# Cross-attention and FFN kernel: dequantisation started at the context maxima over two pairs of PSUM banks

## What is computed

```
q = layernorm(x); k = v = ctx
proj(a, W, b) = a @ W.T + b          -> 16 heads x 8 x 4 ("sup"), for Wq, Wk, Wv (512 x 512)
interfere(a)  = a + 0.1*amp*einsum(a, interference[h])      on the last axis (4)
weights = softmax(q.k / sqrt(8)) per head and sup; out = (weights @ v) @ Wo.T + bo
x = x + out
w_gu = sc[g]*(wq - (zq[g]+1))        4-bit, 512 x 2752, 4 groups
w_d  = the same, 1376 x 512, 10 groups
x = x + (silu(gate)*up) @ w_d        gate, up = layernorm(x) @ w_gu
```

## Time and profile before

| | us |
|---|---|
| median of 3 runs | 906.57 (904.34 to 906.67) |
| the profiled execution | 906.32 |
| its span, first to last instruction | 904.6 |
| mean granted TensorE clock | 0.902 of 2.4 GHz |

### The profile page before, as it was taken

The page is one execution under the profiler, slowest core; times in us unless marked ns, Lnnn a source line. Parts: engine busy times, 40 slices in busy tenths (PEclk is TensorE's granted clock), DMA queues, the critical chain, the costliest instruction groups (busy, mean ns, idle before and its releaser), DMA issues.

```text
span 904.6 us, 23874 instructions
## 1 busy us (share of the span) xinstructions
PE 772.6 (85%) x9953; PEld 562.3 (62%) x9953; DVE 510.2 (56%) x1013; ACT 438.3 (48%) x806; POOL 326.8 (36%) x290
## 2 busy tenths in 40 slices
PE   5306457766799999999999999999999999999898
PEld 5303323322278857876787778677857885787484
DVE  6987745554465646655574556456645663644421
ACT  1426355676365526662555455454635462655120
POOL 6732324555314530543064114412431352144220
PEclk9758655565599999999999999999999999999999
DMA  8900113222101011002100110011001100010000
GB/s 248 292 23 1 50 32 89 69 56 63 32 25 28 3 49 50 3 3 71 28 2 14 60 28 3 13 60 28 2 21 52 28 2 25 3 27 3 24 1 23
DMA packets 20702, 36.98 MB, mean 41 GB/s; under 512 B 3374, under 2 KB 7602, under 8 KB 20592
## 3 DMA queue, kind: packets, MB, share of 16 engines
q1 hardware_dynamic: 20604, 35.48, 13.5%
HBM read 26.56 MB, written 4.19 MB: 34 GB/s over the span
## 4 chain that ended last, share of the span: by engine, by line
PE 67%; DVE 15%; ACT 8%; issue 6%; DMA 2%; SPq 1%; DVEq 0%; ACTq 0%; POOL 0%
PE bank L511 16%; PE bank L526 13%; PE bank L482 9%; PE bank L492 9%; PE bank L644 4%; DVE nmf L1166 4%; PE bank L638 3%; PE bank L661 3%; ACT arena L849 3%; PE bank L619 2%; PE bank L459 2%; DVE arena L1094 2%; DMA arena<-in_L_xattn_Wo 2%; DVE arena L985 2%; PE bank L443 2%
## 5 line engine op out<-in xcount | busy, mean ns | idle before, releaser
L511 PE MATMUL bank<-arena,WGU 128*128 128x256 f16 (+1 forms) x2112 | 247.0, 274 | 1.4 <-DVE arena L709 1.4
L511 PEld LDWEIGHTS bank<-arena,WGU 128*128 128x128 f16 (+1 forms) x2112 | 206.2, 100 | 27.5 <-DVE arena L709 1.6
L1368 POOL TENSOR_TENSOR arena<-arena 128x512 f16<-128x512 f32 x128 | 147.0, 1173 | 190.5 <-ACT arena L856 190.5
L482 PE MATMUL bank<-arena,WT 128*128 128x256 f16 x768 | 91.3, 281 | 40.4 <-DVE arena L709 39.1
L526 PE MATMUL bank<-WD,arena 128*128 128x512 f16 (+1 forms) x528 | 121.1, 379 | 0.0
L849 ACT ACTIVATE arena<-bank,small 128x512 f32<-128x512 f32 x128 | 89.1, 776 | 58.3 <-PE bank L644 58.3
L1355 POOL TENSOR_TENSOR arena<-arena 128x512 f16<-128x512 f32 (+1 forms) x48 | 51.7, 1077 | 172.2 <-ACT arena L829 172.2
L482 PEld LDWEIGHTS bank<-arena,WT 128*128 128x128 f16 x768 | 76.9, 101 | 54.6 <-issue 43.1
L492 PE MATMUL bank<-WT,arena 128*128 128x512 f16 x384 | 88.0, 387 | 1.8 <-DVE arena L707 1.8
L526 PEld LDWEIGHTS bank<-WD,arena 128*128 128x128 f16 (+1 forms) x528 | 49.4, 98 | 53.2
L1166 DVE TENSOR_REDUCE nmf<-bank 128x8 f32<-128x512 f32 x128 | 79.4, 682 | 4.4 <-PE bank L619 4.2
(11 more groups left out here) (157 smaller groups left out, 1068.8 us busy)
## 6 DMA issues: line engine op xcount, KB each, us to landing
arena<-in_L_ffn_qweight_gu SPq DMA_DIRECT2D x8, 688.0 KB, 5.4
arena<-arena SPq DMA_DIRECT2D x32, 144.0 KB, 3.0
WT<-in_ctx SPq DMA_DIRECT2D x8, 512.0 KB, 15.1
arena<-in_ctx SPq DMA_DIRECT2D x8, 512.0 KB, 3.7
arena<-in_x SPq DMA_DIRECT2D x8, 512.0 KB, 3.6
out_y<-arena SPq DMA_DIRECT2D x16, 256.0 KB, 2.1
arena<-in_L_ffn_qweight_down SPq DMA_DIRECT2D x10, 256.0 KB, 3.4
arena<-in_L_xattn_Wk SPq DMA_DIRECT2D x1, 1024.0 KB, 6.6
```

The costliest lines, as they stand in the source:

```text
L482: mm = e.matmul(jb[:, g2 * TOK:(g2 + 1) * TOK], WT[:, w, sp, kb, g * P:(g + 1) * P], src[:, mp, kb, :], start=(n == 0), stop=(n == 11))
L511: mm = e.matmul(pb[0:m, i * TOK:(i + 1) * TOK], WGU[:, sp, kb, half * INTER + fb * P:half * INTER + fb * P + m], x2T[:, mp, kb, :], start= ...
L1368: e.tensor_tensor(phl[:, a, 1, :], pring[:, a, :], phl[:, a, 0, :], ALU.subtract).then_inc(S["p_lo"], 1)
```

## The change

What each part does:

1. **Where the units run.** ND + 5 = 40 ticks. Twenty come early, at new places: one each after the fourth, sixth and eighth context maximum (ctx4, ctx6, ctx8), three at `scales`, two each at `w0` and `w1`, five each at `keys` (after the K projection) and `values` (after the V rows). The other twenty stay in slots: one in each of slots 0 and 1, four in each batch (slot positions 0, 2, 3, 3), two at the end.
2. **Lags.** VectorE does int(n) and w(n - 3), TensorE unit n - 2, ScalarE scaled(n - 2) and hi(n - 4), GpSimd conv(n) and lo(n - 5).
3. **Banks.** The first TWO_PAIRS = 17 units alternate between GB/UB and the JB pair, and wait for `d_w` one unit less. The folds then use only the four AB banks, one after the other.
4. **Conversion** of the integers to bf16 moves from ScalarE to GpSimd (`pool_dequant_conv`).
5. **Wide tables.** The gate/up scales and zero points are loaded over 128 and 32 partitions, split there by VectorE, and written to their table rows by 12 + 4 DMAs from SBUF to SBUF. `dve_zeros` and the gate/up parts of `act_scale_part` are gone.
6. **Own scales for dequantisation.** The maxima of the two scale inputs are reduced by a PARTITION_ALL_REDUCE of their own, early (`MXQ`, `MRQ`); the large one remains.
7. **Reordering of Wo** moves from VectorE to ScalarE. The gate/up one-hot moves from GpSimd to VectorE; the down one-hot stays on GpSimd, in four parts around a subtraction.
8. The order of the loads on SyncE changes.

```diff
-TICKS = ND + 3
-FIRST_SLOT = 2
-TICK_ENDS = [0] * FIRST_SLOT + [TICKS * (k + 1) // (SLICES - FIRST_SLOT) for k in range(SLICES - FIRST_SLOT)]
+TICKS = ND + 5
+TICKS_AT = {"ctx4": 1, "ctx6": 1, "ctx8": 1, "scales": 3, "w0": 2, "w1": 2, "keys": 5, "values": 5}
+BATCH_TICKS = [0, 1] + [slot[j] for slot in IN_BATCH for j in (0, 2, 3, 3)] + AT_TAIL[:2]
+TWO_PAIRS = sum(TICKS_AT[p] for p in PLACES[:PLACES.index("values") + 1]) - 3
...
+            e.wait_ge(S["sc_zeroed"], 2)
+            e.wait_ge(S["wide_ready"], 1)
+            for i in range(PARTS):
+                for g in range(GROUPS_GU):
+                    e.dma_start(sc3_gu[32 * i + g:32 * i + g + 1, :], sc3w[32 * g:32 * g + 32, i, :]).then_inc(S["sc_table"], 16)
+            e.wait_ge(S["zwide_ready"], 1)
+            for g in range(GROUPS_GU):
+                e.dma_start(z_gu[g:g + 1, :], zw[8 * g:8 * g + 8, :]).then_inc(S["z_table"], 16)
+            for c in range(4, NCHUNK):
+                load_ctx_max(e, c)
...
+            for place in ("ctx4", "ctx6", "ctx8", "scales"):
+                pe_ticks(e, place)
+            e.wait_ge(S["fold_evicted"], 4)
+            for t in range(TILES):
+                pe_transpose_tile(e, -1, f"cT{t}", cin, S["ctx_loaded"], 16)
+            pe_ticks(e, "w0")
+            pe_ticks(e, "w1")
...
+            return (JB[0], JB[1]) if n < TWO_PAIRS and n % 2 == 0 else (GB, UB)
...
-            reached(e, S["d_w"], n)
+            reached(e, S["d_w"], n - 1 if n < TWO_PAIRS else n)
...
                 pe_project(e, 1, 1, AB[1], cxT)
             if first:
+                pe_ticks(e, "keys")
                 e.wait_ge(S["wlo_done"], 2)
                 for t in range(TILES):
                     pe_rows(e, 2, t, AB[2 + t], cxT, S["proj_done"])
+                pe_ticks(e, "values")
...
+            for place in ("ctx4", "ctx6", "ctx8", "scales"):
+                act_ticks(e, place)
             e.wait_ge(S["scale_ready"], 1)
             act_whi(e, 0)
             act_hi(e, -1, "cT0"), act_hi(e, -1, "cT1")
+            act_ticks(e, "w0")
             act_whi(e, 1)
+            act_ticks(e, "w1")
...
             for c in range(NCHUNK):
                 e.wait_ge(S[f"ctxm_loaded{c}"], 16)
                 ins = e.tensor_reduce(MXC[:, c:c + 1], cmax_st[:, c], AX_X, ALU.max, apply_absolute_value=True)
+                if c in (3, 5):
+                    dve_ticks(e, f"ctx{c + 1}")
...
+            for n in ticks(place):
+                dve_dequant_int(e, n)
+                dve_dequant_w(e, n - 3)
...
+            e.wait_ge(S["maxq_ready"], 1)
+            e.partition_all_reduce(MRQ, MXQ, P, ABSMAX).then_inc(S["maxq_all"], 1)
+            e.wait_ge(S["sc_high"], 1)
+            e.tensor_tensor(rest_d[0:96, :], scd[0:96, :], sc3_d[0:96, :], ALU.subtract).then_inc(S["sc_rest"], 1)
+            e.wait_ge(S["sc_high"], 2)
+            for i in range(4):
+                pool_hot_d(e, i)
+                if i == 1:
+                    e.tensor_tensor(rest_d[0:64, :], rest_d[0:64, :], sc3_d[0:64, :], ALU.subtract).then_inc(S["sc_rest"], 1)
+            for place in ("ctx4", "ctx6"):
+                pool_ticks(e, place)
             e.wait_ge(S["max_ready"], 1)
             e.partition_all_reduce(MR, MX, P, ABSMAX).then_inc(S["max_all"], 1)
+            pool_ticks(e, "ctx8")
             pool_ln(e, "x", 0)
...
+            for n in ticks(place):
+                pool_dequant_conv(e, n)
+                pool_dequant_lo(e, n - 5)
```

More of the change, by code:

```diff
@@ L83, with ticks @@
 PARTS = 3
-TICKS = ND + 3
-FIRST_SLOT = 2
-TICK_ENDS = [0] * FIRST_SLOT + [TICKS * (k + 1) // (SLICES - FIRST_SLOT) for k in range(SLICES - FIRST_SLOT)]
-def ticks(slot):
-    return range(TICK_ENDS[slot - 1] if slot else 0, TICK_ENDS[slot])
+TICKS = ND + 5
+PLACES = ["ctx4", "ctx6", "ctx8", "scales", "w0", "w1", "keys", "values"] + list(range(SLICES))
+TICKS_AT = {"ctx4": 1, "ctx6": 1, "ctx8": 1, "scales": 3, "w0": 2, "w1": 2, "keys": 5, "values": 5}
+BATCH_TICKS = [0, 1] + [slot[j] for slot in IN_BATCH for j in (0, 2, 3, 3)] + AT_TAIL[:2]
+assert sum(TICKS_AT.values()) + len(BATCH_TICKS) == TICKS
+TICKS_AT.update((k, BATCH_TICKS.count(k)) for k in BATCH_TICKS)
+TWO_PAIRS = sum(TICKS_AT[p] for p in PLACES[:PLACES.index("values") + 1]) - 3
+def ticks(place):
+    before = sum(TICKS_AT.get(p, 0) for p in PLACES[:PLACES.index(place)])
+    return range(before, before + TICKS_AT.get(place, 0))
 def width(block):
@@ L189, in build @@
         eye4 = take(16, F32)
+        early = [take(2048, F32) for _ in range(KB)]
+        bvx = take(2048, F32)
+        inter_all, inter_own, own = early[0][:, 0:HEADS * SUP * SUP], early[0][:, 256:512], early[1][:, 0:4 * SUP]
+        zraw_d = early[1][:, 4 * SUP:4 * SUP + DM // 8].bitcast(U32)
+        zint_d, scd = early[2].bitcast(U32), early[3]
+        rest_d = take(2048, F32)
         wop = [take(2048, F32) for _ in range(KB)]
-        bvx = take(2048, F32)
-        inter_all, inter_own, own = wop[0][:, 0:HEADS * SUP * SUP], wop[1][:, 0:HEADS * SUP * SUP], wop[2][:, 0:4 * SUP]
         take, pos = carver(max(pos[0], body0_end))
@@ L247, in build @@
         BMASK = small[:, 108:124].rearrange("p (w v k) -> p w v k", w=2, v=2)
+        MXQ, MRQ, BDQ, SCQ = (small[:, 124 + 2 * i:126 + 2 * i] for i in range(4))
         GM = small[:, 100:101]
@@ L539, in ffn_slice @@
                 if first:
-                    for n in ticks(k):
-                        pe_dequant(e, n - 1)
+                    pe_ticks(e, k)
                     return
@@ L833, in act_slot @@
             if first:
-                for n in ticks(k):
-                    act_dequant(e, n)
+                act_ticks(e, k)
             else:
@@ L869, in act_chunk @@
                 act_whi(e, 2)
+                act_ticks(e, "keys")
             else:
@@ new lines, in dve_ticks, with dve_zeros_d @@
+        def dve_ticks(e, place):
+            for n in ticks(place):
+                dve_dequant_int(e, n)
+                dve_dequant_w(e, n - 3)
+        def dve_zeros_d(e):
+            e.wait_ge(S["z_loaded"], 16)
+            for k in range(8):
+                ins = e.tensor_scalar(ap(zint_d, 0, GROUPS_D, k, [(8, DM // 8)]), zraw_d[0:GROUPS_D, :], 4 * k, 15,
+                                      ALU.logical_shift_right, ALU.bitwise_and)
+            link(e, ins)
+            e.tensor_scalar(z_d[0:GROUPS_D, 0:DM], zint_d[0:GROUPS_D, 0:DM], -1.0, -1.0, ALU.mult, ALU.add).then_inc(S["zd_ready"], 1)
@@ L1155, in dve_slot @@
             if first:
-                for n in ticks(k):
-                    dve_dequant_int(e, n)
-                    dve_dequant_w(e, n - 1)
+                dve_ticks(e, k)
             else:
@@ L1358, in pool_slot @@
             if first:
-                for n in ticks(k):
-                    pool_dequant_lo(e, n - 3)
+                pool_ticks(e, k)
             else:
@@ L1370, in pool_chunk @@
         def pool_chunk(e, c, first=False, last=False):
+            if first:
+                pool_ticks(e, "keys")
+                e.wait_ge(S["bo_loaded"], 16)
+                e.wait_ge(S["wlo_done"], 3)
+                pool_xres(e, 0)
+                pool_ticks(e, "values")
             pool_slot(e, c, 0, first)
```

277 lines of the change are left out of this document (161 added, 116 removed).

## The result

The changed kernel takes 915.39 us against 905.84 us for the kernel before in the same series. That is the median of four executions, 914.57, 915.12, 915.67 and a slow one of 1954 us, which the ratio leaves out. The ratio is 1.0104, with a 95% interval of 1.0084 to 1.0125: a small difference, but clear of noise. The profiled execution took 914.57 us, 8.25 us more than that of before, and its span is 912.8 us.

The account below looks back on a forecast made before the run. TensorE bounds the kernel from the first Wo; before it, waits between engines decide. Setup -2.9, to K +11.8, to Q +19.0, to scores +5.6, batches -26.4: +7.1 on 906.32 gives 913.4 us; range 895 to 926, the forecast's own 909 to 918.

Parts of the forecast that it names:

- K to Q: From K to Q projection: 45.2 us for 26.2, with ten units added and 0.4 us a unit for port locks.
- The later stretch and the frame: From the first Wo on, TensorE is nearly full and untouched: 664.3 us kept; everything to win or lose lies before.
- The reordering on ScalarE: Setup: the 32 Wo copies cost ScalarE 0.2 us each, 6.4 us, and take 14.4 us off VectorE.
- The chain of GpSimd: Setup: configuration changes around all-reduces cost 7.1 us each, three on the path; second all-reduce at 51.2, scale_ready at 57.0.
- rival 1: GpSimd before the second all-reduce: configuration changes cost nothing, scale_ready at 46.4, total 902.7 us; chance 17%.
- The last fold is out at about 44, at most 52: Setup: with ScalarE's Wo copies after the third fold's copies, the last fold leaves at about 44 us, at most 52.
- Two pairs of banks don't help here: scale_ready to K (22.0 us for 10.1): no help, since engines run in order and w comes a tick late.
- Q to scores and the batches: Q to first scores 18.1 us for 12.5, with two units between; the four batches 105.1 us for 131.5.
- the one unit of slot 0 waits for a w behind the maxima: Start of each batch: from maxima to the unit's turn 5.7 us against 6.2 before, so no gain.
- ring of 3.2 us for units 17 to 34: Sign: units 17 to 34 still take the 3.2 us round of TensorE, ScalarE and VectorE; under 2.3 us in keys.
- Rival 2: Batches and after Q: units cost their busiest engine's 1.8 us, not 3.2; up to 20 us saved, 896 us; chance 13%.
- rival 4: GpSimd's conversions and low parts lock VectorE's ports, 1 us a unit more over ten; reload up to 12 us; 925 us; 14%.

Follow-up runs that it names:

- x6: The kernel before with only the 32 copies that reorder Wo moved to ScalarE: 893.10 us, ratio 0.9862.
- x2: The changed kernel with the early all-reduce of the scale inputs' maxima replaced by a memset constant: 918.54 us, ratio 1.0143 to the kernel before.
- x10: x1 with the scale inputs' maxima in the large all-reduce, and gate/up one-hot, scales and conversions 0 and 1 behind it: 920.38 us, ratio 1.0159 to before.
- x1: The changed kernel with ScalarE's second down-scale part after the first fold's copies, not before the bias copies: 911.41 us, ratio 1.0062 to the kernel before.
- x4: The changed kernel with all units on one pair of banks (TWO_PAIRS = 0): 936.32 us, ratio 1.0333 to the kernel before.
- x14: The changed kernel with VectorE doing w(n - 2) instead of w(n - 3) in the slots: 887.85 us, ratio 0.9800 to the kernel before.
- x5: The changed kernel with the conversion of the integers on ScalarE instead of GpSimd: 923.24 us, ratio 1.0191 to the kernel before.
- x7: The changed kernel with the ten ticks of keys and values, and their piece loads, back in the slots: 928.25 us, ratio 1.0254 to the kernel before.
- x13: x7 with w(n - 2) instead of w(n - 3) in the slots: 893.00 us, ratio 0.9854 to the kernel before.
- x11: x10 with eight small zero-point shifts moved behind the context maxima and rstd ahead of the scales ticks: 911.76 us, ratio 1.0052 to the kernel before.
- x12: x11 with w(n - 2) instead of w(n - 3) in the slots: 884.10 us, ratio 0.9754 to the kernel before.

## Why the prediction was right, and where its working was not

The forecast of 913.4 us, slower, held (915.39; the profiled execution 914.57), and the mechanism that it names, early units that cost more ahead of Q than they save in the batches, is what the stretches show. That it came within 2 us is in part luck: K came 4.6 us later than forecast and the stretch from K to Q was 3.6 us shorter, and two of its signs, the first high part at 62 to 64 and K at 77 to 81, failed (67.75 and 83.57). Step by step:

- **The later stretch and the frame.** 663.2 us against 664.3. Right.
- **The reordering on ScalarE.** 0.2 us a copy; it took 6.51 us for 32. Right. x6 prices the part at 12.6 us.
- **The chain of GpSimd.** Three stalls ahead of the second all-reduce, predicted at 50.8 to 51.2, came at 51.89, and `scale_ready` at 58.41 for 57.0. Right, and rival 1 with its price of nothing per stall fell. But that such a stall is pure loss, as its sum has it, fell too, in x2 and x10.
- **"The last fold is out at about 44, at most 52".** Wrong, 57.9. The step "they start after the third fold's copies" took the folds' own start as in the trace of before and did not follow what the bias copies had been put behind. VectorE's maxima came at 43.8 for 38. The price was a first high part at 67.75 for 62.7, 3 to 4 us in the end by x1.
- **"Two pairs of banks don't help here"**, before K. Wrong: 10.3 us by x4. The time of that stretch was worked out from the waits that the code has with two pairs, and it holds (15.8 us from the first high part to K, for 16.3; the 3 us too few to K come from the late folds). The remark drawn from it does not: with one pair, units 3 to 7 each wait for a product one unit younger.
- **K to Q**, predicted 45.2, measured 41.6. Mechanism right, and the sum 3.6 us too high. The two long waits are where it had them (5.8 us ahead of 95.81, 5.0 ahead of 114.63, for 5.8 and 4), but between them the units start at 95.81, 97.29, 98.99 and 100.78, and at 114.63, 115.71 and 117.24: 1.1 to 1.8 us apart, where 1.7 and 0.4 for the locks were costed.
- **Q to scores and the batches**, 18.1 and 105.1 predicted, 17.9 and 106.4 measured. The times are right, and so is the mechanism of slot 0 ("the one unit of slot 0 waits for a w behind the maxima"). Batch by batch, from scores to scores, 25.5, 22.9, 26.4 and 30.3 were predicted and 25.0, 27.4, 25.6 and 28.4 came: the second, in which the chain of conversion, rstd and product shown above stands, was forecast 4.5 us too short, and the other three made most of that good, which is luck. Its sign "ring of 3.2 us for units 17 to 34" held only for pairs such as 163.78 and 166.96; the next units start 6.2, 9.7 and 7.9 us later (173.12, 182.86, 190.79). What the prediction did not do is to ask where the sentence on slot 0 comes from. It counted the four maxima as something that a unit in slot 0 has to wait for. They are that only because of part 2 of the change, the lag of 3, which I read as part of how two pairs of banks work and costed at nothing by itself. x14 prices it at 27.5 us: with it away the same change is 18.7 us faster than before, not 9.6 us slower.
- **Rival 2**, that the units hide beside the attention, had 13%. Its size, 20 us, was nearly that of x14, but its mechanism is not the one that x14 shows: one unit of a batch hides behind the maxima there, the others still stand 3.2 us or more apart and not 1.8. (Its bounds are also miscounted: 10 to 20 us off 913.4 is 893 to 903, not 901.)
- **Conversions on GpSimd** (the sentence on locks, and rival 4). x5 shows no price of theirs in the slots, 2 us gained from K to Q, and a gain in the setup.

In sum, by single edits: the reordering brings 12.6 us in the kernel before; moving ten ticks ahead of Q brings 12.9 us as the change has it (x7 against after) and 5.2 us with the right lag (x13 against x14); the scale part ahead of the bias copies costs 4; the lag in the slots costs 27.5 and is by itself more than the whole loss.

## What to carry to other kernels

When a pipeline is given more stages because it gets more buffers, look at the places where the buffers are not there: a lag chosen for two pairs of banks put every product one tick late where there was one pair, behind whatever else the engine does between ticks. Price each lag by what stands in the queue between "its input is ready" and "its turn comes". A stage time that comes out as predicted does not show that the stage had to cost that much; compare it with the stage before for the work in it (here 144.0 us for 38 ticks against 154.2 for 30 in x7, the same attention in both), and if the new one takes longer for less, find the wait that is new.

## What the runs showed of the hardware that was not expected

- The stall of about 7 us around a PARTITION_ALL_REDUCE goes both ways (9.02 and 6.98 us into it, 7.28 and 6.93 out of it; the 9.02 overlap a wait for VectorE), but the conversion (CAST) right behind one does not pay it, in the changed kernel, x10 or x11; the first TENSOR_TENSOR behind does. The GPSIMD Engine Reference of the Trainium skill (Instruction dispatch) gives about 6 us for the first call to a freshly loaded kernel. The trace agrees in size. The changed kernel has a pair of MODIFY_POOL_CONFIG at each of its four changes between the two kinds, not only at the first, and where no other wait covered the stall it took 5.74 (x2) to 7.12 us (x14) into the large all-reduce and 6.85 (x7) to 7.90 us (x6) out of one.
- VectorE's small shifts beside GpSimd wait for one whole GpSimd instruction after another: eight of 10 x 64 took 12.43 us in x10, the length of three such instructions, and 0.91 us alone in x11. Its maxima beside the same GpSimd work did not lengthen (4.47 us for two in the changed kernel, and as much in x2 with GpSimd idle).
- Who gets the ports first can go either way: x11 and x12 have the same instructions up to the slots, and the eight shifts of L1136 took 8.24 us in one and 6.47 us in the other, the product behind them 5.04 and 3.14, with the all-reduce 4.9 us apart. These are two single executions; x11's own four lie between 910.23 and 914.94 us, and whether the same draw is behind that is not shown.
- With the waits gone the batches ran at a mean granted clock of 0.63 instead of 0.55, and TensorE was busy 51.0 us instead of 54.4 with the same matmuls. So of the 27 us at most 3.4, by this difference in busy time (an estimate), come from TensorE's clock.
